# Another order of head and row in two DRAM scratch tensors, and row counts of the transfers around them

## The reference, cut to what matters

```
q = _rope((x @ Wq.T).reshape(B, S, H, d)); k = _rope((x @ Wk.T)...); v = (x @ Wv.T)...
gate = einsum('bshd,bnhd->bhsn', q, k.reshape(B, nblk, 32, H, d).mean(axis=2))
sel  = top 4 blocks of the gate (own block always, later blocks never)
scores = einsum('bihd,bjhd->bhij', q, k) * d ** (-0.5), NEG where not (sel and causal)
o = softmax(scores) @ v
s = (o * rsqrt(mean(o * o) + EPS) * o_norm_w) @ Wo.T
```

## Time and profile before

| | |
|---|---|
| median of 3 runs | 425.1 us (425.1, 422.94, 425.44) |
| profiled execution, its own time | 423.56 us |
| its span, first to last instruction | 421.8 us |
| busy, share of the span | PE 82%, DVE 71%, POOL 42%, ACT 40% |
| DMA queue q1 (SP) | 18.80 MB in 12946 packets |
| DMA queue q10 (ACT) | 11.01 MB in 4032 packets |

### The profile page before, as it was taken

One profiled execution on the slowest core, in us unless ns is written; L12 is line 12 of the kernel. 1 busy time (PEld: TensorE's weight loads), 2 busy tenths in 40 slices (PEclk: granted clock), 3 DMA queues, 4 the chain that ended last, 5 costly groups with the idle time before them and its releaser, 6 DMA issues. The chain is left out here.

```text
span 421.8 us, 6060 instructions
## 1 busy us (share of the span) xinstructions
PE 345.8 (82%) x2028; PEld 239.9 (57%) x2028; DVE 301.4 (71%) x857; ACT 170.8 (40%) x305; POOL 175.2 (42%) x121
## 2 busy tenths in 40 slices
PE   0697767567779989999999999999673988997981
PEld 0585555455546656676666666666572775444641
DVE  3867489867997877894554764683759959558694
ACT  1422553461224322226454454644112667757610
POOL 7654283463444642554255636565445000000023
PEclk9999689698999999999999999999985889998798
DMA  8200168976897311211211141110008000000011
GB/s 273 69 23 20 50 159 175 167 139 168 184 159 125 89 47 42 73 37 53 70 39 39 40 137 39 39 37 2 1 2 262 3 2 0 0 1 0 2 50 50
DMA packets 17009, 30.20 MB, mean 72 GB/s; under 512 B 3140, under 2 KB 12012, under 8 KB 16556
## 3 DMA queue, kind: packets, MB, share of 16 engines
q1 hardware_dynamic: 12946, 18.80, 20.0%
q10 hardware_dynamic: 4032, 11.01, 8.8%
HBM read 24.99 MB, written 4.82 MB: 71 GB/s over the span
## 5 line engine op out<-in xcount | busy, mean ns | idle before, releaser
L390 POOL TENSOR_TENSOR wl<-wr,wh 128x768 fp32r<-128x768 f32 x28 | 51.4, 1835 | 66.1 <-ACT wh L476 50.2
L532 ACT ACTIVATE PT<-bank 128x512 f32<-128x512 f32 (+1 forms) x88 | 44.3, 557 | 38.1 <-PE bank L955 38.0
L689 DVE TENSOR_REDUCE mx<-bank 128x1 f32<-128x384 f32 (+3 forms) x88 | 52.2, 636 | 6.6 <-PE bank L937 6.4
L149 PE MATMUL bank<-xh,wh 128*128 128x512 f32 x112 | 50.6, 452 | 4.4 <-DVE gb L814 1.4
L428 POOL TENSOR_TENSOR gl<-gb,gh 128x512 fp32r<-128x512 f32 x28 | 36.5, 1303 | 36.3 <-DVE gh L821 23.7
L151 PE MATMUL bank<-xh,wl 128*128 128x512 f32 x112 | 45.6, 407 | 0.0
L150 PE MATMUL bank<-xl,wh 128*128 128x512 f32 x112 | 45.4, 406 | 0.0
L936 PE MATMUL bank<-KS,QS 112*128 112x128 bf16 (+3 forms) x128 | 32.5, 305 | 13.3 <-DVE mx L689 7.5
L1216 POOL TENSOR_TENSOR left<-xn,x 128x256 f32<-128x256 f32 x8 | 7.0, 898 | 87.1 <-DVE xn L1443 87.1
L149 PE MATMUL bank<-wh,gh 128*128 128x256 f32 x112 | 37.1, 331 | 0.5 <-POOL gl L428 0.5
L539 ACT ACTIVATE th<-bank 128x512 f32<-128x512 f32 x28 | 16.7, 596 | 45.7 <-PE bank L151 45.7
(11 more groups left out here) (235 smaller groups left out, 837.6 us busy)
## 6 DMA issues: line engine op xcount, KB each, us to landing
wr<-in_w_chunks_dram ACTq DMA_DIRECT2D x28, 384.0 KB, 3.2
KS<-parts_dram SPq DMA_DIRECT2D x12, 256.0 KB, 8.7
parts_dram<-wp SPq DMA_DIRECT2D x12, 128.0 KB
QS<-parts_dram SPq DMA_DIRECT2D x2, 768.0 KB
parts_dram<-x SPq DMA_DIRECT2D x12, 128.0 KB
w_ai<-in_w_ai_dram SPq DMA_DIRECT2D x1, 1152.0 KB, 5.5
x<-in_x_dram SPq DMA_DIRECT2D x2, 512.0 KB, 6.4
QS<-parts_dram SPq DMA_DIRECT2D x2, 512.0 KB
```

What stands on the lines that cost most here:

```text
L149: pe.matmul(out, l_hi, r_hi, start=start, stop=False, skip_group_check=skip)
L390: pool.tensor_tensor(wl[:, s % 3, :, :], wr[:, s % 2, :, :], wh[:, s % 3, :, :].bitcast(F32), ALU.subtract).then_inc(wl_ready, 1)
L532: act.activation(PT[:, k % 8, 0:n], bank[k % 2][:, 0:n], ACT.Exp, scale=float(DH) ** -0.5).then_inc(P_ready, 1)
L689: dve.tensor_reduce(mx[:, b * TB + i, heads[0]:heads[-1] + 1], bank[k % 2][:, 0:len(heads) * n].rearrange("p (h n) -> p h n", n=n), AX.X, ...
```

## The change

Three things change, all in transfers of layer 0.

1. `parts_dram` and `bias_dram` are laid out with the head outside the row: (head, dimension, token) and (head, block, token) where they had (dimension, head, token) and (block, head, token). A write of 128 partitions then goes to 128 adjacent rows of 1 KB. A read of 16 partitions takes for each partition 16 pieces of 1 KB, 16 KB apart, where it took one of 16 KB.
2. The query stack is read in six transfers of 16 partitions, as the key stack is, where it was read in three of 48, 32 and 16. `BLOCKS` names the levels of the six blocks.
3. The key constants are loaded for each batch in two transfers, of 16 and of 3 partitions, where one had 19.

The counts that PE waits for follow. No instruction of PE, DVE, ACT or POOL changes, except those counts.

```diff
--- before.py
+++ after.py
@@ -47,6 +47,7 @@
 STEPS = HALVES * CH
 SENT, SENT_TEST = 3e38, 1e38
 STACK = [(0, 0), (0, 1), (1, 0), (1, 1), (0, 2), (2, 0)]
+BLOCKS = [(level, first) for first in range(3) for level in range(3 - first)]
 R_BIAS = len(STACK) * DH
 R_MAX = R_BIAS + NBLK
 R_ALL = R_MAX + 3
@@ -240,8 +241,8 @@
         bank = [m.ps(f"bank{i}") for i in range(8)]
         bank_b = [bank[i][:, :].bitcast(BF16) for i in range(8)]
 
-        parts_dram = nc.dram_tensor("parts_dram", (B, 2, 3, DH, H, S), BF16, kind="Internal").ap()
-        bias_dram = nc.dram_tensor("bias_dram", (B, NBLK, H, S), BF16, kind="Internal").ap()
+        parts_dram = nc.dram_tensor("parts_dram", (B, 2, 3, H, DH, S), BF16, kind="Internal").ap()
+        bias_dram = nc.dram_tensor("bias_dram", (B, H, NBLK, S), BF16, kind="Internal").ap()
         max_dram = nc.dram_tensor("max_dram", (B, 3 * H, S), BF16, kind="Internal").ap()
 
         x_in = [m.sem(f"x_in{b}") for b in range(B)]
@@ -310,16 +311,18 @@
 
             sp.dma_start(wo[:, :, :], a["w_o"].rearrange("(k p) n -> p k n", p=P)).then_inc(sem_wo, 16)
             for b in range(B):
-                sp.dma_start(KS[R_BIAS:R_ALL, b, :, :],
-                             spread(a["c_kconst"][:, b * S:(b + 1) * S], 1, H)).then_inc(kconst_ready, 16)
+                for rows in (slice(R_BIAS, R_MAX), slice(R_MAX, R_ALL)):
+                    sp.dma_start(KS[rows, b, :, :],
+                                 spread(a["c_kconst"][rows.start - R_BIAS:rows.stop - R_BIAS, b * S:(b + 1) * S], 1, H)
+                                 ).then_inc(kconst_ready, 16)
 
             def stack_bias(b):
                 sp.wait_ge(biasT_read, b + 1)
                 for f in range(2):
-                    sp.dma_start(bias_dram[b, :, f * 8:(f + 1) * 8, :].rearrange("n h t -> h n t"),
+                    sp.dma_start(bias_dram[b, f * 8:(f + 1) * 8].rearrange("h n t -> (h n) t"),
                                  biasT[:, f, :]).then_inc(bias_out, 16)
                 sp.wait_ge(bias_out, 32 * (b + 1))
-                sp.dma_start(QS[R_BIAS:R_MAX, b, :, :], bias_dram[b]).then_inc(q_stacked[b], 16)
+                sp.dma_start(QS[R_BIAS:R_MAX, b, :, :], bias_dram[b].rearrange("h n t -> n h t")).then_inc(q_stacked[b], 16)
 
             def stack_parts(b, halves):
                 for k in halves:
@@ -327,25 +330,20 @@
                     which, half = k // 2, k % 2
                     for level, done in enumerate((H_ready, M_ready, L_ready)):
                         sp.wait_ge(done, n + 1)
-                        sp.dma_start(parts_dram[b, which, level, :, half * 8:(half + 1) * 8, :].rearrange("d h t -> h d t"),
+                        sp.dma_start(parts_dram[b, which, level, half * 8:(half + 1) * 8].rearrange("h d t -> (h d) t"),
                                      parts[n % 4][:, level, :]).then_inc(parts_out[n % 4], 16)
                     if half == 0:
                         continue
 
                     sp.wait_ge(parts_out[(n - 1) % 4], 48 * (b + 1))
                     sp.wait_ge(parts_out[n % 4], 48 * (b + 1))
-                    src = parts_dram[b, which].rearrange("l d h t -> (l d) h t")
-                    row = 0
-                    for first in range(3):
-                        count = 3 - first
-                        rows = slice(row, row + count * DH)
+                    src = [parts_dram[b, which, level].rearrange("h d t -> d h t") for level in range(3)]
+                    for block, (of_q, of_k) in enumerate(BLOCKS):
+                        rows = slice(block * DH, (block + 1) * DH)
                         if which == 0:
-                            sp.dma_start(QS[rows, b, :, :], src[0:count * DH]).then_inc(q_stacked[b], 16)
+                            sp.dma_start(QS[rows, b, :, :], src[of_q]).then_inc(q_stacked[b], 16)
                         else:
-                            for r in range(row, row + count * DH, DH):
-                                sp.dma_start(KS[r:r + DH, b, :, :], src[first * DH:(first + 1) * DH]
-                                             ).then_inc(k_stacked[b], 16)
-                        row += count * DH
+                            sp.dma_start(KS[rows, b, :, :], src[of_k]).then_inc(k_stacked[b], 16)
 
             def stack_maxima(b):
                 sp.wait_ge(maxT_read, b + 1)
@@ -922,9 +920,9 @@
 
                 b, g, r = k // (NG * LOADS), k // LOADS % NG, k % LOADS
                 if g == 0 and r == 0:
-                    pe.wait_ge(q_stacked[b], 16 * (3 + 1))
+                    pe.wait_ge(q_stacked[b], 16 * (len(BLOCKS) + 1))
                     pe.wait_ge(k_stacked[b], 16 * len(STACK))
-                    pe.wait_ge(kconst_ready, 16 * B)
+                    pe.wait_ge(kconst_ready, 32 * B)
                 i, heads = unit_loads(g)[r]
                 n = (i + 1) * P
                 if k < 2:
@@ -944,7 +942,7 @@
                 j, heads = exp_loads(w % NG)[r]
                 n = S - j * P
                 if w % NG == 0 and r == 0:
-                    pe.wait_ge(q_stacked[b], 16 * (3 + 2))
+                    pe.wait_ge(q_stacked[b], 16 * (len(BLOCKS) + 2))
                 if k == 0:
                     pe.wait_ge(A_read, B * NG * LOADS)
                 if k >= 2:
```

## The result

| | before | changed |
|---|---|---|
| median, 20 runs each | 423.82 us | 425.87 us |
| lowest to highest | 421.81 to 429.74 | 424.04 to 429.06 |
| profiled execution, its own time | 423.56 us | 424.12 us |
| its span | 421.8 us | 422.3 us |

The ratio is 1.0049, 95% interval 1.0025 to 1.0072: 2.05 us slower, where I had forecast 0.9 us faster. The time lies inside the range; the direction is wrong. An execution that took over 1.5% more than the fastest of its kernel is left out of this and all later ratios.

What follows compares the result with a forecast made beforehand. The prediction took the DMA chain ending in the bias read, for which PE waits 4.3 us at pass A, as the bound. Writes save 3.8 us, query reads lose 2.9: 424.3 - 0.9 = 423.4 us, range 420.0 to 427.5.

Steps and rivals of the forecast that it cites:

- What bounds the kernel: Start of pass A, batch 0: PE waits 4.3 us for the bias read, DVE idles 3.6, behind a 38.1 us DMA chain.
- Writes of parts: Key, query and bias writes as 128 adjacent rows: all 16 engines, twice the pace, 3.8 us saved with issue time.
- Reads of the key stack and of the bias: In the chain: if 16 destination rows (first case) set the 122 GB/s, 1 KB pieces change nothing; costed at 0.
- Reads of the query stack: In the chain: six narrow reads at 122 GB/s replace wide ones at 157, 12.9 us for 10.0, costing 2.9 us.
- Key constants and batch 1: Constants' loading from 25 to 40 us is hidden; batch 1's bias read has 5.3 us of room; each worth 0.
- Rival C: Chain reads: 1 KB pieces into 16 rows slow them to 96 GB/s, 6.7 us lost, 431.0 us; chance 0.19.
- B: Chain reads: sources now 1 KB apart speed them up, the stall is gone, 420.7 or 420.0 us; chance 0.27.
- D: Writes stay on eight engines, only the query reads' 2.9 us loss remains, 427.2 us; chance 0.06.
- Share near 1 in the key writes: Sign for the writes: DMA share near 1.00 during the key writes, with loads beside it, where it was 0.50.
- Second landing within 18 us: Sign for the writes: key writes, landed at 77.02 before, land about 18 us after the query reads' issue or less.
- forecast A: The forecast itself: writes on 16 engines, narrow reads at 122 GB/s, 423.4 us; chance 0.48.
- PE's wait: Sign at pass A's start, line 936, waiting for `QS`: 3.4 us in A, none in B, 6 to 11 in C.

Runs made afterwards that it cites:

- `e5_spread`: The changed kernel with destination rows of each 16-row transfer six apart (row d of block i at partition 6d + i); ratio 0.9975 to the kernel before.
- `e3_narrow`: The kernel before with only the query stack read in six transfers of 16 partitions, still in 16 KB pieces; ratio 1.0043.
- `e12_narrow_writes`: The changed kernel without its 1 KB pieces, bias and constants as before: six narrow query reads and part writes as 128 rows; ratio 1.0039 to the kernel before.
- `e1_consts`: The kernel before with only the key constants loaded as 16 and 3 rows; ratio 1.0003.
- `e10_qpieces`: The kernel before with the query stack read in six transfers of 16 rows, these alone in 1 KB pieces; ratio 1.0092.
- `e11_kpieces`: The kernel before with six query reads of 16 rows in 16 KB pieces, and the key reads in 1 KB pieces; ratio 1.0082.
- `e6_again`: Repeat of the kernel before, its layout and writes kept, with destination rows six apart and the query stack read in six transfers; ratio 0.9950.
- `e2_writes`: The kernel before with only the part writes as 128 adjacent rows, bias writes as before; ratio 0.9962.

## Why the prediction was wrong

**What bounds the kernel: right.** The one wait, its place and its chain are in both profiles. Spreading the rows changed only the reads of the stacks, took the wait away and gave 0.5%: 2.1 us, interval 0.5 to 3.7. The 3.6 us of DVE were the bound, and `e5_spread`, at most 2.8 us faster than before, stayed under it.

**Writes of parts: right in kind, its size failed.** "I take it that all 16 engines carry it, at twice the pace" was right in direction: alone, the share rose from 0.52 to 0.80 and six writes took 4.18 us in place of 6.97. But I took the time of the writes from the bytes: 4.6 us for the key writes, of which half goes. In the chain six narrow reads take 14.88 us by themselves and 18.30 with the key writes behind them: the writes cost 3.4, not 4.6, and 1.7 as 128 rows. By that subtraction part of the writing went on beside the last reads. It is worse with the bias writes: 15.70 less 14.88, so 0.8 us where I had 1.5, and the saving is 0.2 to 0.5 where I had 0.8 and 0.3 for the issue. The 3.8 us, or 3.4 without the last query write's 0.4, which is outside this chain, were 1.9 alone and 2.1 with loads. In the kernel, behind narrow reads, they were fewer still: 0.2 us between `e3_narrow` and `e12_narrow_writes`, not clear of noise. This term, the saving of the writes, is the step that failed most.

**Reads of the key stack and of the bias: the pace right, the price of the pieces wrong.** That the 16 destination rows set the pace is shown. "In the first case the new pieces change nothing" did not follow from it. GB/s over a window, 121 against 122, could not show it: 0.5 us in 15 is 3%, no more than a window's edges and a load beside it change. And the pieces are in the query reads too, where my term counted only their width.

**Reads of the query stack: right.** 2.9 forecast, 2.4 to 2.6 measured alone, 1.8 in the kernel.

**Key constants and batch 1: right**, nothing each. The bias read of batch 1 was issued at 135.68 us and no engine waited for a DMA there.

**The sum.** 3.8 saved less 2.9 lost was 0.9 us saved. With what the chain measured it is about 2.0 saved, 2.6 lost and 0.5 to 1.4 for the pieces: 1.1 to 2.0 us lost, or 0.4 less with the last query write, against 2.05 (1.05 to 3.05) in the runs. The mistakes were 1.3 to 1.5 us in the writes and 0.5 to 1.4 in the pieces and had one sign; the terms were of nearly equal size and opposite, so the sign of the sum hung on them. That the time stayed inside the range owes nothing to the sum: the range was wide enough for both signs. Rival C had the sign and the cause ("pieces of 1 KB into 16 rows") but priced it from a transfer on a single engine, at 96 GB/s: 7.6 us for the pieces (35.5 less 27.9), at least five times too much. Its point of decision, 118 GB/s, was computed with the 3.8 us; with 2.0 saved the reads may take 27.0 us, which is 126 GB/s, and the 122 counted on was on the losing side. B was refuted and D too.

**The signs.** Share near 1 in the key writes: 0.88, but 0.34 of it was the weight load, so the sign proved little. Second landing within 18 us: missed, 19.83. The sign was also drawn wrong: by the prediction's own terms the link is 18.4 + 2.9 - 2.3 = 19.0 us, so a landing at 18 never belonged to forecast A. PE's wait: 5.4, between the 3.4 of A and the 6 of C; `e1_consts` shows that this wait moves by 2.7 us with the chain unchanged, so it could not part them.

**What stays open.** Why pieces cost more behind or ahead of the old writes (2.0) than of the new ones (1.4), and why loads make them cheaper. How much the writes and how much the pieces cost in the kernel itself: `e12_narrow_writes` puts most of it on the writes, the chain alone splits it. Why `e10_qpieces` and `e11_kpieces` measured as much as both together: their profiled chains were longer too, by 4.7 and 3.5 us, but for the second the excess over `e3_narrow` lies mostly in a link that its edit did not touch.

## What to carry to other kernels

Before reading a transfer's gain from bytes and GB/s, ask what it runs behind: what queues behind a slow read is partly hidden by it, and only the difference of two links tells its price. Before reading GB/s of a stretch as the pace of one transfer, split it by queue: here 131 of 314 GB/s belonged to a load on another queue. Where a forecast is the difference of two nearly equal terms, a mistake in the size of either, or a small term costed at nothing, decides the sign; here it was the writes first and the cut of rows into 1 KB pieces second. And if 16 rows of SBUF set the pace, no other layout of DRAM helps, but another layout of the destination does: with rows six apart a stack took 9.11 us in place of 14.88, with nothing else changed.

## What the runs showed of the hardware

- Transfers into 16 adjacent partitions ran at about 120 GB/s with all 16 DMA engines occupied. While those into 16 partitions six apart ran, 224 and 242 GB/s moved in all (`e5_spread`, `e6_again`, 60 to 67 us; 16 of the 242 on ACT's queue). Alone, a stack took 14.88 us and 9.11.
- Pieces of 1 KB in place of 16 KB cost 0.5 us for 1.57 MB alone, at either spacing of the rows. The Trainium skill (DMA: Bandwidth & Descriptors, "Specifications") lets line rate begin at 512 B; here 1 KB is 3 to 5% dearer than 16 KB.
- 19 rows of constants took 14.3 us a transfer alone (190.83 to 219.46 for two), 16 and 3 rows 5.5.
- A load on ACT's queue moved nothing while SP's reads filled the engines: issued at 64.37 us in the kernel before, the 384 KB landed 10.1 us later, and from 62 to 69 us all 1.10 MB were SP's.
- The time of this kernel goes with the mean granted clock: over all runs 0.30 us less for each 0.001 (runs of the kernel before average 426.1 us at 0.924, 423.5 at 0.931, 422.3 at 0.935; correlation -0.82 in 110 of them). Which of the two causes the other is not shown. By a fit at equal clock the changed kernel is 2.4 us slower than before (1.9 to 3.0), the spread ones 2.2 to 3.3 us faster, `e10_qpieces` 4.1 and `e11_kpieces` 1.9 us slower, and `e2_writes` only 0.4 us faster, which is not clear of noise (0.7).
